# Three kept samples with y made early, their scaling shared with VectorE, and the last sample but one stored in parts

## The chip, the core and the metric

The kernel runs on one core of a Trainium2 chip. The metric is the device time of one execution in microseconds (us), that of the kernel before: 1872.82, 1877.70 and 1878.64 us in three runs, median 1877.7.

## What is computed

The input x is 32 samples of 256 channels with 56 x 56 = 3136 pixels, float32 (3136 KB a sample). Two layers follow one another, here cut to what matters:

```python
# layer 0: rotate the channels, quantise to 8 bits over ALL samples, rotate back
im = relu(x) as (256, all pixels); mn = mean(im); p = u.T @ (im - mn); p = clip(p, -cv, cv)
q  = round((p - min(p)) * 255 / (max(p) - min(p)))      # min, max per channel, over all samples
y  = u @ dequantised(q); y = y - mean(y) + mn
# layer 1: an attention weight per sample and channel, from a covariance
h = relu(w1 @ y * g + b); d = relu(w_dr @ h * g + b)    # 256 -> 256 -> 128 channels
cov = covariance of d over the sample's pixels           # 128 x 128
att = sigmoid(w_fc @ (rows of cov weighted by w_row) + b_fc)
out = y * att
```

Minimum, maximum and mean run over all 32 samples, so that nothing of layer 1 can begin before all of p is known and quantised. The output needs y twice over: once folded into h (the kernel multiplies w1 by u beforehand and works on q alone), and once as itself, scaled by att.

## The kernel before, in words

There are three stages, each a block of its own with a program for each engine.

**Stage 1** (to 564 us) computes p for all samples, with minimum and maximum. 28 samples go to a scratch in DRAM; the last four (RES = 4, the kept samples) stay in SBUF as `p_res[:, 0..3]`.

**Stage 2** (564 to 772 us) quantises p once to get the mean of q. The 28 samples come back from DRAM as 56 tiles of 128 x 3136 float32 (a channel half each, 1568 KB), through four buffers `pt`. SP loads a buffer again as soon as VectorE has quantised it (L431 to L441). VectorE quantises a tile (L633), ScalarE sums it (L525). The four kept samples are quantised too, and their q is kept as bytes (`q_kept`). Pairs of samples are numbered i = 0..13, the tiles of a pair t = 0..3. Beside this, TensorE makes y of two kept samples (MADE = 2) ahead of time, in chunks of the pixels: CH = 7 chunks of a sample with 512, 512, 512, 512, 384, 384 and 320 columns. A list `Y_PLACES` (L393) says after which tile VectorE does the work for the next chunk: `keep_y(j - 1)` copies the chunk before from PSUM to `p_res` in two halves (L606), `halve(j)` turns the bytes of chunk j into float16 for TensorE (L599). VectorE waits in `keep_y` for TensorE's eight matmuls of the chunk (L502).

**Stage 3** (from 772 us) runs the second layer, sample after sample: the four kept ones first, in the order of `ORDER`, then the 28 from DRAM, which are quantised again. A phase is one sample, with seven steps s = 0..6, one chunk each. The text counts the phases 0, 1, 2 and so on; phases 6 and later are a loop. The engines of a step work on different chunks, and each engine's order is written out:

- TensorE: z of chunk s (8 matmuls, L1024), y of the chunk 11 steps back, that is of the sample before (8 matmuls, L998), d of chunk s-1 (L949), covariance of chunk s-2 (L931). In step 1 the covariance comes right behind z. In step 4 the logits (L1009).
- ScalarE: gg of chunk s-2 (L1066), h of chunk s in two halves (L1074), hh (L1079), in step 4 the sigmoid and the scales `att_cy` (L1087, L1092), then y times att in two halves (L1112).
- VectorE: conversion of chunk s+2 (L1128, with the quantisation L1135 ahead of it for samples from DRAM), low half of g (L1182), in steps 1, 2 and 3 the small work of the covariance and the attention weights (L1210 to L1245), g (L1172) and low half of h (L1160).
- SP: in step 4 the store of a sample whose seven chunks are done (L891), and loads of the samples from DRAM.

Where y of a chunk was made in stage 2 (`made(o)`), TensorE leaves it out and ScalarE scales it in place, from SBUF to SBUF. For two made samples these are steps 4 to 6 of phase 1, all of phase 2 and steps 0 to 3 of phase 3. On such steps VectorE does g ahead of the low half of h (`has_no_y`, L1246).

The last sample has its y (`final_output`, L965) in three PSUM buffers, the first three chunks of it ahead of its logits; ScalarE and VectorE scale a half each, and SP stores chunk by chunk (L895 to L897). The sample before it is stored whole, in step 4 of phase 32 (L891).

## Time and profile before

| | |
|---|---|
| median of three runs | 1877.7 us (1872.82 to 1878.64) |
| the profiled execution | 1876.54 us, span 1874.8 us |
| TensorE busy | 90% of the span |
| VectorE busy | 83% |
| ScalarE busy | 79% |
| TensorE's mean granted clock | 0.944 of 2.4 GHz |
| DMA | 477.38 MB, 255 GB/s over the span |
| the chain that ended last | TensorE 55% of the span, VectorE 2%, ScalarE 1% |

The rows below come from the page of the profiled execution and from its trace. The chain is the chain of waits that ended last. A window is a stretch of the span, given with the busy time of each engine in it. A row of the timeline is one instruction or a few alike, with the idle time before it and what ended it in square brackets.

### The profile page before, as it was taken

The numbers are of one execution on the slowest core, as the hardware profiler recorded it, in microseconds if no ns is written. First come the engines' busy times: TensorE is split into PE (matmuls) and PEld (weight loads), VectorE is DVE, ScalarE is ACT, GpSimd is POOL, SyncE is SP. The second block draws the span as 40 slices with busy tenths as digits, with TensorE's granted clock in tenths as the row PEclk, the third lists the DMA queues.
The fourth block names the chain that finished last, engine by engine and source line by source line (L and its number), as shares of the span: only waits on it lengthen the run. The fifth ranks groups of instructions, "written<-read, shape, count | busy, mean of one in ns | idle before, by whom it ended". The sixth has DMA issues, their size and how long they took to land.

```text
span 1874.8 us, 40122 instructions
## 1 busy us (share of the span) xinstructions
PE 1693.6 (90%) x13394; PEld 1319.7 (70%) x13394; DVE 1558.2 (83%) x2855; ACT 1489.5 (79%) x2265; POOL 460.6 (25%) x136
## 2 busy tenths in 40 slices
PE   8999999999993034489999999999999999999998
PEld 8999999999992011366666666666666666666665
DVE  6888888888887787678888888888888888888885
ACT  7777777777768997689878878888788788887885
POOL 7888888888870000000000000000000000000000
PEclk9999999999995556699999999999999999999999
DMA  9998998999999999503546546455464464554635
GB/s 338 372 376 304 375 365 315 373 351 328 374 356 386 429 431 429 231 2 148 170 158 236 169 173 219 158 211 189 156 235 168 174 217 159 213 188 154 235 116 207
DMA packets 140592, 477.38 MB, mean 255 GB/s; under 512 B 10624, under 2 KB 33536, under 8 KB 125568
## 3 DMA queue, kind: packets, MB, share of 16 engines
q1 hardware_dynamic: 140544, 476.75, 68.9%
q8 instruction: 28, 0.46, 0.1%
q14 instruction: 20, 0.16, 0.0%
HBM read 284.04 MB, written 192.68 MB: 254 GB/s over the span
## 4 chain that ended last, share of the span: by engine, by line
PE 55%; DVE 2%; ACT 1%; issue 1%; ACTq 0%; DVEq 0%
PE z_ps L1024 17%; PE y_ps L998 16%; PE d_ps L949 14%; PE cov_ps L931 5%; PE ch_ps L1009 1%; DVE hl L1160 0%; ACT p_res L1112 0%; DVE g L1172 0%; PE ch_ps L962 0%; PE ch_ps L961 0%; DVE gg L1182 0%; ACT h L1074 0%; PE y_ps L978 0%; ACT gg L1066 0%; PE cov_ps L934 0%
## 5 line engine op out<-in xcount | busy, mean ns | idle before, releaser
L299 POOL TENSOR_TENSOR xl<-early,xh 128x1568 fp32r<-128x1568 f32 x128 | 459.7, 3592 | 96.1 <-ACT xh L258 96.1
L1024 PE MATMUL z_ps<-qr,wh 128*128 128x512 f16 (+2 forms) x896 | 315.4, 355 | 0.0
L1024 PE MATMUL z_ps<-qr,wl 128*128 128x512 f16 (+2 forms) x896 | 315.4, 355 | 0.0
L1160 DVE TENSOR_TENSOR hl<-h,hh 128x1024 f16<-128x1024 f32 (+2 forms) x224 | 243.9, 1089 | 79.8 <-ACT hh L1079 79.5
L258 ACT ACTIVATE xh<-early 128x1568 fp32r<-128x1568 f32 x128 | 194.2, 1517 | 139.1 <-PE pp L316 139.0
L949 PE MATMUL d_ps<-vh,hh 128*128 128x128 f16 x1600 | 281.1, 220 | 3.5 <-DVE hl L1160 3.3
L998 PE MATMUL y_ps<-qr,udh 128*128 128x512 f16 (+2 forms) x812 | 283.9, 353 | 0.0
L998 PE MATMUL y_ps<-qr,udl 128*128 128x512 f16 (+2 forms) x812 | 283.6, 352 | 0.0
L1074 ACT ACTIVATE h<-z_ps,sb_h 128x512 f32<-128x512 f32 (+2 forms) x448 | 264.4, 626 | 23.2 <-PE z_ps L1024 20.4
L949 PE MATMUL d_ps<-vh,hl 128*128 128x128 f16 x1600 | 281.1, 220 | 0.0
L949 PE MATMUL d_ps<-vl,hh 128*128 128x128 f16 x1600 | 281.0, 220 | 0.0
L316 PE MATMUL pp<-xh,uh 128*128 128x392 f32 x1024 | 267.1, 342 | 9.1 <-ACT xh L258 9.1
L1112 ACT ACTIVATE p_res<-y_ps,att_cy 128x512 f32<-128x512 f32 x406 | 269.6, 713 | 6.5 <-ACT att_cy L1092 5.0
L316 PE MATMUL pp<-xh,ul 128*128 128x392 f32 x1024 | 266.3, 341 | 0.0
L1066 ACT ACTIVATE gg<-g 128x512 f16<-128x512 f32 (+1 forms) x224 | 130.7, 584 | 160.7 <-DVE g L1172 160.5
L350 DVE TENSOR_REDUCE pmin<-pp 128x784 f32 x256 | 248.3, 970 | 0.0
L1079 ACT ACTIVATE hh<-h 128x1024 f16<-128x1024 f32 (+2 forms) x224 | 213.0, 951 | 7.1
L252 ACT ACTIVATE early<-early 128x784 f32<-128x784 f32 x256 | 215.3, 844 | 3.6 <-DMA early<-in_x_dram 3.6
L316 PE MATMUL pp<-xl,uh 128*128 128x392 f32 x1024 | 204.5, 341 | 0.0
L316 PEld LDWEIGHTS pp<-xh,uh 128*128 128x128 f32 x1024 | 188.5, 188 | 9.1 <-issue 9.1
L316 PEld LDWEIGHTS pp<-xh,ul 128*128 128x128 f32 x1024 | 188.6, 188 | 0.0
L316 PEld LDWEIGHTS pp<-xl,uh 128*128 128x128 f32 x1024 | 185.1, 188 | 0.0
(197 smaller groups left out, 2961.1 us busy)
## 6 DMA issues: line engine op xcount, KB each, us to landing
early<-in_x_dram SPq DMA_DIRECT2D x128, 784.0 KB, 6.7
out_dram<-p_res SPq DMA_DIRECT2D x31, 3136.0 KB, 10.2
early<-p_scratch SPq DMA_DIRECT2D x42, 1568.0 KB, 12.8
p_res<-p_scratch SPq DMA_DIRECT2D x112, 512.0 KB, 4.4
p_scratch<-early SPq DMA_DIRECT2D x56, 784.0 KB, 7.7
p_scratch<-late SPq DMA_DIRECT2D x56, 784.0 KB, 7.7
p_res<-p_scratch SPq DMA_DIRECT2D x56, 384.0 KB, 3.2
late_tile<-p_scratch SPq DMA_DIRECT2D x13, 1568.0 KB, 12.8
```

Of the source, the lines that this page charges most:

```text
L252: last = nc.scalar.activation(xs[:, k, m], xs[:, k, m], ACT.Relu, accum_out=xsum[:, m, bass.ds(g, 1)])
L258: nc.scalar.activation(xh[:, k % 2], xs[:, k], ACT.Copy).then_inc(high_done, 1)
L299: nc.gpsimd.tensor_tensor(xl[:, k % 2], xs[:, k], xh[:, k % 2].bitcast(F32), ALU.subtract).then_inc(split_done, 1)
L316: last = nc.tensor.matmul(pp[:, k % 2, m, c, 0:SC], lhs, rhs[:, c * SC:(c + 1) * SC], start=first and n == 0, stop=final and n == len(part ...
L350: nc.vector.tensor_reduce(pmin[:, m, bass.ds(g, 1)], p_psum(k, m), AX_XY, ALU.min).then_inc(psum_read, 1)
L949: last = nc.tensor.matmul(d_ps[:, par, t], lhs, rhs, start=n == 0, stop=n == len(parts) - 1)
L998: last = nc.tensor.matmul(y_ps[:, m, 0:widths[c]], part[:, k, m * P:(m + 1) * P], qr[:, slot, k, columns(c)], start=k == 0 and part is udh ...
L1024: last = nc.tensor.matmul(z_ps[:, m, 0:w], part[:, k, m * P:(m + 1) * P], qr[:, a, k, columns(s)], start=k == 0 and part is wh, stop=k == ...
L1074: nc.scalar.activation(h32[:, par, m, 0:w], z_ps[:, m, 0:w], ACT.Relu, bias=sb_h[:, m:m + 1]).then_inc(z_read, 1)
L1079: nc.scalar.activation(hh[:, par, :, 0:w], h32[:, par, :, 0:w], ACT.Copy).then_inc(hh_done, 1)
L1112: nc.scalar.activation(yo[:, slot, m, columns(c)], y_in, ACT.Identity, scale=att_cy[:, m, 0:1], bias=att_cy[:, m, 1:2]).then_inc(y_free, 1)
L1160: nc.vector.tensor_tensor(hl[:, par, :, 0:w], h32[:, par, :, 0:w], hh[:, par, :, 0:w], ALU.subtract).then_inc(h_split, 1)
```

## The change

- MADE goes from 2 to 3. `ORDER` becomes [1, 3, 2, 0]: y of kept samples 1, 3 and 2 is made in stage 2. `Y_PLACES` gets 22 places from pair 5 to pair 12 (before, 15 were used, from pair 6 to the first tile of pair 12). In pairs 10 and 12 all four tiles are places.
- Made chunks are scaled by ScalarE (first half of the channels) and by VectorE (second half, in place, behind the low half of h). A semaphore `made_scaled` counts VectorE's part; SP waits for it ahead of the store, and ScalarE ahead of the sigmoid, which overwrites `att_cy`.
- A made sample is stored from its place in `p_res`. The first one lies in `p_res[:, 1]`, which is also the buffer of the samples from DRAM (`pc`). So the first seven chunk loads move from the start of stage 3 to phase 2, step 4, behind the store of that sample and a wait for its landing.
- The third chunk of the last sample's y moves behind the logits.
- The last sample but one is stored in three parts (chunks 0 to 2, 3 and 4, 5 and 6), each as soon as it is scaled, and no more whole in phase 32.

```diff
--- before.py
+++ after.py
@@ -389,9 +389,11 @@
         tiles = [tiles_in_all // CH + (c < tiles_in_all % CH) for c in range(CH)]
         starts = [P * sum(tiles[:c]) for c in range(CH)]
         widths = [min(P * t, M - at) for t, at in zip(tiles, starts)]
-        MADE = 2
-        Y_PLACES = [(i, t) for i in range(6, PAIRS) for t in ((0, 2) if i <= 2 * RES else (0, 1, 2))][1:]
-        ORDER = [*range(RES - MADE, RES), *range(RES - MADE)]
+        MADE = 3
+        Y_PLACES = [(i, t) for i in range(5, 2 * RES + 1) for t in (0, 2)] + [
+            (i, t) for i in range(2 * RES + 1, PAIRS - 1) for t in range(3 + (i % 2 == 0))]
+        ORDER = [1, 3, 2, 0]
+        assert len(ORDER) == RES and len(Y_PLACES) > MADE * CH
 
         def columns(c):
             return slice(starts[c], starts[c] + widths[c])
@@ -764,7 +766,7 @@
         cov_centred, r_summed, r_done = sem("cov_centred"), sem("r_summed"), sem("r_done")
         weighted_done = sem("weighted_done")
         logits_done, att_done, attb_done = sem("logits_done"), sem("att_done"), sem("attb_done")
-        y_done, y_free = sem("y_done"), sem("y_free")
+        y_done, y_free, made_scaled = sem("y_done"), sem("y_free"), sem("made_scaled")
         half_free = [sem(f"half_free{m}") for m in range(K)]
 
         with ExitStack() as c_:
@@ -843,6 +845,10 @@
 
                 return not has(r2, a, s, CH + Y_LAG) or made(output_chunk(r2, a, s)[0])
 
+            def kept_y(o, c):
+
+                return p_res[:, ORDER[o // CH], :, columns(c)]
+
             def converted_chunk(r2, a, s):
 
                 return 2 * r2 + a + (s + LEAD) // CH, (s + LEAD) % CH
@@ -864,9 +870,6 @@
             def _(sp):
                 def load(i, c):
                     sp.dma_start(pc[:, :, columns(c)], p0_v[i, :, :, columns(c)]).then_inc(chunk_loaded[c], 16)
-
-                for c in range(CH):
-                    load(0, c)
 
                 def store(n, a, first, end):
 
@@ -878,7 +881,12 @@
                             sp.wait_ge(half_free[m], end)
                     else:
                         sp.wait_ge(y_free, K + K * (CH * n + end))
-                    sp.dma_start(out_v[which, :, :, part], yo[:, a, :, part]).then_inc(out_stored[a], 16)
+                    if isinstance(n, int) and n < MADE:
+                        sp.wait_ge(made_scaled, CH * n + end)
+                        source = p_res[:, ORDER[n], :, part]
+                    else:
+                        source = yo[:, a, :, part]
+                    sp.dma_start(out_v[which, :, :, part], source).then_inc(out_stored[a], 16)
 
                 def phase(r2, a):
                     for s in range(CH):
@@ -887,15 +895,23 @@
                             n, c = converted_chunk(r2, a, s)
                             sp.wait_ge(chunk_quantised, CH * (n - RES) + c + 1)
                             load(n - RES + 1, c)
-                        if s == Y_LAG and exists(r2, a, back=2) and exists(r2, a, back=1):
+                        if s == Y_LAG and exists(r2, a, back=2) and exists(r2, a):
                             store(2 * r2 + a - 2, a, 0, CH)
+                            if isinstance(r2, int) and 2 * r2 + a == 2:
+
+                                sp.wait_ge(out_stored[0], 32)
+                                for c in range(CH):
+                                    load(0, c)
 
                 phases(sp, phase)
 
+                parts_before = [(0, 3), (3, 5), (5, CH)]
+                for first, end in parts_before:
+                    store(N - 2, 0, first, end)
                 last_parts = [(c, c + 1) for c in range(CH)]
                 for first, end in last_parts:
                     store(N - 1, 1, first, end)
-                sp.wait_ge(out_stored[0], 16 * (N // 2) + 16)
+                sp.wait_ge(out_stored[0], 16 * (N // 2 - 1 + len(parts_before)) + 16)
                 sp.wait_ge(out_stored[1], 16 * (N // 2 - 1 + len(last_parts)) + 16)
 
             @block.tensor
@@ -985,7 +1001,7 @@
                     if has(r2, a, s, CH + Y_LAG):
                         o, slot, c = output_chunk(r2, a, s)
                         if final(o):
-                            for n in range(0, 3) if c == 0 else range(c + 2, min(c + 3, CH)):
+                            for n in range(0, 2) if c == 0 else range(c + 2, min(c + 3, CH)):
                                 final_output(FINAL + n, n)
                             return
                         if made(o):
@@ -1038,6 +1054,8 @@
                         if not exists(r2, a):
                             spread(r2, a, s)
                         logits(r2, a, s)
+                        if s == Y_LAG and has(r2, a, s, CH + Y_LAG) and final(output_chunk(r2, a, s)[0]):
+                            final_output(FINAL + 2, 2)
                         reduced(r2, a, s)
                         if s != 1:
                             covariance(r2, a, s)
@@ -1083,6 +1101,8 @@
                             act.wait_ge(logits_done, n)
 
                             act.wait_ge(y_free, K + K * (first_chunk(r2, a) - CH))
+                            if isinstance(r2, int) and 2 <= n <= MADE + 1:
+                                act.wait_ge(made_scaled, CH * (n - 1))
                             for m in range(K):
                                 last = nc.scalar.activation(att[:, m:m + 1], ch_ps[:, 2 * P + m:2 * P + m + 1],
                                                             ACT.Sigmoid, bias=bfc_sb[:, m:m + 1])
@@ -1103,14 +1123,15 @@
                                                      ACT.Identity, scale=att_cy[:, 0, 0:1],
                                                      bias=att_cy[:, 0, 1:2]).then_inc(half_free[0], 1)
                                 continue
+                            if made(o):
+                                kept = kept_y(o, c)[:, 0]
+                                nc.scalar.activation(kept, kept, ACT.Identity, scale=att_cy[:, 0, 0:1],
+                                                     bias=att_cy[:, 0, 1:2]).then_inc(y_free, K)
+                                continue
                             for m in range(K):
-                                if made(o):
-                                    y_in = yo[:, slot, m, columns(c)]
-                                else:
-                                    act.wait_ge(y_done, K * (o - MADE * CH) + m + 1)
-                                    y_in = y_ps[:, m, 0:widths[c]]
-                                nc.scalar.activation(yo[:, slot, m, columns(c)], y_in, ACT.Identity,
-                                                     scale=att_cy[:, m, 0:1],
+                                act.wait_ge(y_done, K * (o - MADE * CH) + m + 1)
+                                nc.scalar.activation(yo[:, slot, m, columns(c)], y_ps[:, m, 0:widths[c]],
+                                                     ACT.Identity, scale=att_cy[:, m, 0:1],
                                                      bias=att_cy[:, m, 1:2]).then_inc(y_free, 1)
 
                 phases(act, phase)
@@ -1246,6 +1267,12 @@
                         if has_no_y(r2, a, s):
                             rectified_g(r2, a, s)
                             low_half_of_h(r2, a, s)
+                            if has(r2, a, s, CH + Y_LAG):
+                                o, slot, c = output_chunk(r2, a, s)
+                                kept = kept_y(o, c)[:, 1]
+                                dve.wait_ge(attb_done, o // CH + 1)
+                                nc.vector.tensor_scalar(kept, kept, att_cy[:, 1, 0:1], att_cy[:, 1, 1:2], ALU.mult,
+                                                        ALU.add).then_inc(made_scaled, 1)
                         else:
                             low_half_of_h(r2, a, s)
                             if has(r2, a, s, CH + Y_LAG) and final(output_chunk(r2, a, s)[0]):
```

## Rows read from the trace of the kernel before

In a row of windows stand: the stretch, its length, the busy time and the instructions of PE, PEld, DVE, ACT and POOL, the granted clock as a share of 2.4 GHz, the DMA share and GB/s.

**Rows 1.** Page, part 2: DMA busy in tenths, 40 slices of the span.
```profile
DMA  9998998999999999503546546455464464554635
```

**Rows 2.** Two windows of stage 2.
```profile
600.00:640.00 40.00, 2.66 (x6) 1.43 (x6) 30.29 (x34) 40.00 (x30) 0.00 (x0) 0.50 1.01 430
...
720.00:740.00 20.00, 10.90 (x35) 3.94 (x36) 17.37 (x20) 14.82 (x11) 0.00 (x0) 0.67 1.01 428
```

**Rows 3.** Timeline of VectorE in stage 2, around one 512-column chunk of y.
```profile
716.35 1.91 DVE L633 TENSOR_SCALAR qt<-early,lo,qa 128x3136 uint8<-128x3136 f32 x1
...
720.02 0.69 DVE L606 COPY p_res<-wfc_ps 128x512 f32<-128x512 f32 x1 [1.01 <-PE wfc_ps L502]
...
721.23 1.91 DVE L633 TENSOR_SCALAR qt<-early,lo,qa 128x3136 uint8<-128x3136 f32 x1
```

**Rows 4.** Timeline of VectorE in stage 2 where no y work is left.
```profile
754.54 1.91 DVE L633 TENSOR_SCALAR qt<-late_tile,lo,qa 128x3136 uint8<-128x3136 f32 x1 [1.80 <-DMA late_tile<-p_scratch]
```

**Rows 5.** Page, part 6: loads of stage 2, KB each, median us to landing.
```profile
late_tile<-p_scratch SPq DMA_DIRECT2D x13, 1568.0 KB, 12.8
```

**Rows 6.** Windows of phases 1 to 4 of stage 3.
```profile
801.31:830.32 29.01, 24.41 (x267) 17.67 (x266) 23.48 (x48) 22.85 (x38) 0.00 (x0) 1.00 0.01 2
830.32:860.50 30.18, 26.22 (x267) 18.83 (x266) 23.59 (x48) 27.85 (x47) 0.00 (x0) 0.94 0.26 107
860.50:893.16 32.66, 30.75 (x291) 20.92 (x290) 26.07 (x53) 29.85 (x49) 0.00 (x0) 0.95 0.36 130
893.16:927.18 34.02, 34.02 (x322) 23.31 (x321) 29.58 (x62) 27.92 (x46) 0.00 (x0) 1.00 0.50 174
```

**Rows 7.** Windows of steps: phase 1 steps 1-3, phase 2 steps 1-3, phase 4 steps 0-3.
```profile
804.45:817.28 12.83, 11.68 (x126) 8.09 (x124) 11.58 (x30) 9.09 (x13) 0.00 (x0) 1.00 0.00 1
...
833.74:848.88 15.14, 13.31 (x124) 9.24 (x123) 11.49 (x30) 13.62 (x21) 0.00 (x0) 0.89 0.00 1
...
893.16:913.09 19.93, 19.93 (x189) 13.45 (x187) 17.66 (x43) 15.99 (x24) 0.00 (x0) 1.00 0.34 96
```

**Rows 8.** The chain of waits in phase 2, steps 0 to 2: start, us, what.
```profile
834.81 0.87 ACT p_res L1112 x2
...
836.21 0.52 ACT gg L1066
...
838.01 2.49 PE d_ps L949 x24
```

**Rows 9.** Group by shape: ScalarE scales made halves, phases 1 to 3.
```profile
L1112 ACT ACTIVATE p_res<-p_res,att_cy 128x512 f32<-128x512 f32 x16 | 12.1, 802 | 0.1
```

**Rows 10.** Group by shape: VectorE quantises 512 columns, from phase 4 on.
```profile
L1135 DVE TENSOR_SCALAR q<-p_res,lo,qa 128x512 uint8<-128x512 f32 x212 | 105.6, 540 | 0.0
```

**Rows 11.** Windows: 3.4 us of phase 2 at the lower clock; the end.
```profile
838.20:841.60 3.40, 3.40 (x27) 2.58 (x25) 1.68 (x6) 2.30 (x4) 0.00 (x0) 0.50 0.02 5
1850.00:1855.00 5.00, 4.91 (x36) 2.88 (x32) 2.51 (x11) 3.60 (x6) 0.00 (x0) 1.00 0.01 2
1857.00:1872.00 15.00, 9.46 (x53) 5.02 (x51) 5.74 (x9) 5.64 (x11) 0.00 (x0) 1.00 1.03 411
```

**Rows 12.** The chain of waits at the end: start, us, what.
```profile
1858.81 1.73 PE d_ps L978 x8
1860.54 0.35 PE ch_ps L1009 x4
...
1865.91 1.30 PE d_ps L978 x8
1867.21 1.10 PE y_ps L978 x8
...
1868.33 0.61 DVE p_res L1257
```

**Rows 13.** Timeline of SP: its last issue, the last chunk's store.
```profile
1869.02 0.70 SPq L881 DMA_DIRECT2D out_dram<-p_res  x1
```

**Rows 14.** DMA issues at the end: that store's KB and us to landing.
```profile
out_dram<-p_res SPq DMA_DIRECT2D x1, 320.0 KB, 5.3
```

## What is predicted, and why

> **What bounds the kernel now.** I read the page's slices first. The DMA share tells the stages apart: about 9 tenths in stages 1 and 2, about 5 in stage 3 [rows 1]. Then windows by stage. In stage 2 the DMA engines are busy without a break at 429 GB/s while TensorE has much idle time; ScalarE is fully busy for a while, but later it is not and the DMA still is [rows 2]. Where no y work is left, VectorE waits 1.80 us for each tile [rows 4]. So stage 2 ends when 28 samples have been read, and work on VectorE there is free as long as no load is issued late. In stage 3 the windows by phase show two regimes [rows 6]. From phase 4 on TensorE is busy for the whole 34.02 us of a phase: it is the bound. In phases 1 to 3, where y has been made, TensorE is busy only 24.4 to 30.8 us of 29.0 to 32.7. There the chain of waits goes round the engines: ScalarE's scaling of made y (L1112), behind it gg, behind that VectorE and TensorE's d [rows 8]. At the end the chain is TensorE, the logits, the scaling, and the DMA engines are saturated from 1857 to 1872 after standing nearly idle before 1855 [rows 11].
>
> **The third made sample: what TensorE saves.** Y of a 512-column chunk takes TensorE 1.73 us, of a 384 one 1.30, of the 320 one 1.10 [rows 12]. A sample is 4 x 1.73 + 2 x 1.30 + 1.10 = 10.6 us of matmuls that leave stage 3. But a phase without y does not get 10.6 us shorter: phase 2 takes 30.2 us against 34.0 of phase 4 [rows 6]. So the question is how long made phases are after the change, when ScalarE scales one half instead of two.
>
> **ScalarE and VectorE in made steps.** A half of 512 columns costs ScalarE 0.80 us by duration [rows 9]. One half goes, so gg, h and hh of the next step start some 0.75 us earlier. VectorE gets an operation the trace does not have: 128x512 float32, SBUF to SBUF, two scalars per partition. The nearest row is the quantisation of the same shape from the same memory, 0.54 us [rows 10]; as such operations overlap at their edges, I take 0.45 from start to start. The bounds are 0.3 and 0.8, the latter being what ScalarE takes for this shape [rows 9]. The row's 0.54 us is for float32 read and bytes written. The Trainium skill, VectorE: DVE Perf Modes, section "The perf-mode tier table", gives a one-source float32 operation within SBUF the doubled rate, 1227 ns for 2048 elements; by it an estimate for 512 is some 0.35 us, and the sum would be 1 to 2 us better than mine.
>
> Now the steps. In steps 1 to 3 VectorE also has the covariance work. Phase 1 shows these three steps with no scaling of y at all: 12.83 us, VectorE busy 11.58 of them, so VectorE is nearly the bound [rows 7]. Phase 2, with both halves on ScalarE, has 15.14, part of it at the lower clock (0.89 in the mean) [rows 7]. After the change I take 12.83 + 3 x 0.45 = 14.2. The other four steps of phase 2 were 30.18 - 15.14 = 15.0; the shorter ScalarE should give 0.3 of it. A made phase then takes 28.9 us.
>
> Phase by phase, against [rows 6]:
> - Phase 1 has three steps with made chunks, and ScalarE is shorter in them: 29.0 to 28.3.
> - Phase 2: 30.2 to 28.9.
> - Phase 3 becomes fully made, but its last two steps have the first quantisations of a sample from DRAM, 2 x 2 x 0.45 = 1.8 us on VectorE [rows 10], of which I charge 1.4: 32.7 to 30.3.
> - Phase 4: its first four steps lose y, and TensorE's 19.93 us would fall by 4 x 1.3 to 1.7. But VectorE is busy for 17.66 us of them [rows 7]; with four more operations of 0.54 that is 19.8, so VectorE takes over as the bound and nearly nothing is won: 34.0 to 33.9.
>
> Together 125.9 us become 121.4, a gain of 4.5 us. The steps of phase 1 that I built on ran at the full clock, those of phases 2 and 3 had a fall to the lower clock each (means 0.94 and 0.95) [rows 6]. In one such stretch the granted clock was 0.50 for 3.4 us, that is 1.2 GHz, behind a stall of TensorE, and 24 matmuls of d took 2.49 us [rows 8, 11]. I charge one fall, 1.2 us (at most half of 3.4, 1.7, less what the waits absorb). Stage 3's body: -3.3 us; between -7 (no fall, the cheap operation) and +1 (three falls, the dear one).
>
> **What the seven more chunks cost in stage 2.** Each brings VectorE one L599 and two L606, about 1.9 us, 13 us in all. The cover is the DMA: a tile takes 1568 KB at 429 GB/s = 3.74 us, and VectorE quantises it in 1.9 [rows 2 to 4]. Where places follow one another without a gap, VectorE also waits for TensorE at the lower clock: the row pair shows a tile with a 512-column chunk taking 721.23 - 716.35 = 4.9 us, 1.0 of it waiting [rows 3]. That is 1.15 us late per such tile; 384- and 320-column chunks are about even. In pair 10 to 12 there are up to seven places in a row; walking through them with these numbers VectorE is up to 3.1 us late at tile (11,3) and on time again in pair 13. How late may it be? A load lands 12.8 us after its issue, three others being ahead of it [rows 5]; so the DMA engines have 3 x 3.74 - 1.9 = 9.3 us of work left when VectorE is on time. 3.1 is well under that. I take 0.5 us for unevenness among the DMA engines, bounds 0 and 3.
>
> **What is moved on SP.** The seven chunk loads leave the start of stage 3, where nothing waits for them, and now stand behind the store of the first made sample and a wait for its landing. Behind that wait on SP are those loads and the store in phase 3, step 4. The store begins in step 4 of phase 2, takes about 11 us, the loads 3.2 MB / 429 GB/s = 7.5 and seven issues; VectorE wants the first chunk in step 5 of phase 3, a phase and a step later, some 32 us. Slack over 10 us: nothing. The cover gone, each us late would stall VectorE and then TensorE. ScalarE's new wait ahead of the sigmoid: behind it stand the sigmoid and the scaling, then gg. VectorE's last half of step 3 ends before ScalarE's hh of step 4, so nothing.
>
> **The end.** With the third final chunk behind the logits, these start 1.73 us earlier [rows 12]; its y is still ready when the third scaling wants it. Everything to the last scaling (1868.33 + 0.61) moves by 1.7. The last store was issued at 1869.02 and landed 5.3 us later, at 1874.3 [rows 13, 14], because the DMA engines still had the whole of sample 30 to write at 1857 [rows 11]. In parts, more than half of it goes into the idle time before 1855. The last sample alone needs 3.2 MB / 411 GB/s = 7.8 us from about 1862: to 1870, plus the landing's tail of some 2 us. Gain 2.3 us, between 1.5 and 3.5.
>
> **The sum**, against the profiled execution (1876.54; span 1874.8): -3.3 + 0.5 - 2.3 = -5.1, that is 1871.4. The median of the runs is 1.2 above that execution, their mean 0.1 below it; I lay half between and say 1872.0. About 0.3% (5.6 us) is what a measurement of this kernel can tell from no change, and my gain is right at it.
>
> **The rivals.**
> 1. The gain is eaten in the made phases. TensorE's clock is at 0.50 where it had stalled [rows 8, 11], and the change makes a third phase of that kind. The Trainium skill says so too, TensorE: Matmul & The Clock Gate, section "HAM oscillation — how this bites in real kernels": waits between bursts of matmuls bring the clock down again and again; the trace agrees, with 3.4 us at 0.50. With a fall in each of three phases (3.6 us) and VectorE's operation at 0.8, the body gives +0.5, the end -2.3, stage 2 +0.5: 1875. For it: both whole made phases before had a fall. Against: the stall that came ahead of it hangs on ScalarE's second half.
> 2. Nearly all goes well: no fall, the cheap operation, the end at 3.5: -10 us, 1867. Against it: VectorE's 17.66 of 19.93 us in phase 4.
> 3. Slower: stage 2 turns from DMA-bound to VectorE-bound. If VectorE's lateness in pairs 9 to 12 passes 9.3 us, buffers are freed too late, the DMA engines run dry, and each further place costs its full 1.9 us: up to 13 us for seven, less the 5.6 of the rest: +7, 1884. Against it: the walk ends at 3.1.
> 4. The split of the work does not show: made phases stay at 30.2 since another chain (hl to d to g to gg) is as long, while the rest is as forecast: 1875 as well. I count it with the first.
>
> **How the numbers follow.** Forecast 0.55 (its own range 1869 to 1875.5), rivals 1 and 4 0.25, rival 2 0.13, rival 3 0.07. The range to be given reaches from 1866.5 to 1877.5; it takes in rivals 1, 2 and 4 and leaves out rival 3 and the edges. Faster by over 0.3% (below 1872.1): rival 2 and somewhat over half of the forecast, 0.45. Slower by over 0.3%: rival 3 and little else, 0.07. Same: 0.48.
>
> **What would show it.** Windows of the phases: made phases 28 to 29.5, phase 4 about 34 with VectorE at 0.9 and more in its first steps. L599 and L606 seven and fourteen more, stage 2 no longer, the DMA share still 1.01 in pairs 9 to 12. The logits 1.7 us earlier against the end of the last d, the last store landing some 3 us after its issue. The prediction is wrong if the DMA share falls in stage 2, if VectorE waits for a chunk load in phase 3, or if made phases stay over 30 us.

## The result

The changed kernel takes 1867.77 us in the median of nine runs (1865.97 to 1869.84), the kernel before 1875.35 in its nine (1872.32 to 1880.25). The ratio is 0.9952, 95% interval 0.9942 to 0.9962: some 9 us, between 7 and 11; the two medians are 7.6 us apart. Forecast were 5.7 us from a median of 1877.7, that is 1872.0, with 0.48 of the chance on no difference that can be measured. The sign of the forecast sum was right, its size too small, and the largest single chance lay on "same", where the time did not come out. The measured 1867.8 us lies outside the forecast's own range (1869 to 1875.5) and inside the range given (1866.5 to 1877.5) only because that took in the second rival.

The profiled execution of the changed kernel has a span of 1866.5 us, 8.3 less than that of before. First the page, granted clock, DMA share and groups of the chain:

```profile
PEclk9999999999996567699999999999999999999999
DMA  9998998998999999405546546455465464554535
```
```profile
PE 51%; DVE 4%; ACT 0%; issue 0%; DVEq 0%; ACTq 0%
```

The stages are as in [rows 1]. In the chain ScalarE has gone and VectorE has come up from 2 to 4%. Now the windows of phases 1 to 4 in the changed kernel, columns as in [rows 6]:

```profile
802.03:830.47 28.44, 24.40 (x266) 17.65 (x265) 24.38 (x50) 22.22 (x37) 0.00 (x0) 1.00 0.01 2
830.47:858.74 28.27, 24.49 (x268) 17.73 (x266) 26.04 (x55) 23.29 (x40) 0.00 (x0) 1.00 0.26 110
858.74:889.05 30.31, 24.47 (x266) 17.71 (x265) 28.01 (x59) 23.99 (x40) 0.00 (x0) 1.00 0.61 228
889.05:922.71 33.66, 29.61 (x292) 20.11 (x290) 31.96 (x68) 25.94 (x42) 0.00 (x0) 1.00 0.53 185
```

Together 120.7 us against 125.9 in [rows 6], 5.2 less. The clock column (TensorE's granted clock as a share of 2.4 GHz) reads 1.00 in all four, where it read 0.94 and 0.95 in phases 2 and 3: there the clock had fallen to 0.50 for 3.4 us each time. Such a stretch is called a fall below. VectorE is busy 32.0 of 33.7 us in phase 4. The steps that answer to [rows 7] are phase 2 steps 1 to 3 and phase 4 steps 0 to 3:

```profile
833.62:847.41 13.79, 11.84 (x125) 8.10 (x123) 12.58 (x32) 11.06 (x17) 0.00 (x0) 1.00 0.00 1
889.05:908.14 19.09, 15.34 (x157) 10.25 (x155) 18.71 (x45) 13.94 (x20) 0.00 (x0) 1.00 0.41 122
```

The new operation, by shape (busy us, mean ns), where [rows 10] had stood in for it:

```profile
L1274 DVE TENSOR_SCALAR p_res<-p_res,att_cy 128x512 f32<-128x512 f32 x12 | 6.5, 543 | 0.5 <-ACT att_cy L1112 0.5
```

The end, as the chain of waits (start, us, what), for [rows 12]; SP's issues of the first and the last chunk of sample 31, for [rows 13]; and the last store's size and us to landing, for [rows 14]:

```profile
1854.45 0.35 PE ch_ps L1025 x4
...
1856.62 1.90 PE y_ps L994 x8
...
1861.13 1.10 PE y_ps L994 x8
...
1862.25 0.61 DVE p_res L1284
```
```profile
1856.68 0.37 SPq L889 DMA_DIRECT2D out_dram<-p_res  x1
...
1862.94 0.37 SPq L889 DMA_DIRECT2D out_dram<-p_res  x1
```
```profile
out_dram<-p_res SPq DMA_DIRECT2D x1, 320.0 KB, 3.1
```

From the logits to the end of the span are 1866.5 - 1854.45 = 12.05 us; before, 1874.8 - 1860.54 = 14.26. And from the first z of phase 5 to the logits are 931.74 us against 933.36. So the end gives 1.6 + 2.2 = 3.8 us.

The 8.3 us then are: start of stage 3 at 775.28 instead of 774.91, +0.4; phase 0 26.75 instead of 26.40, +0.3 (both vary by 2 us and more between traces whatever the change, see the section on stage 2); phases 1 to 4 -5.2; the end -3.8.

### The profile page after: what moved, and what is told of

Read it like the earlier page. It is cut to its first block, busy times and chain, and to the rows that moved or that the text cites. A ratio compares the mean times of both kernels' runs of the same rounds, so it can differ in the third digit from the quotient of the medians.

```text
span 1866.5 us, 40162 instructions
## 1 busy us (share of the span) xinstructions
PE 1695.2 (91%) x13394; PEld 1317.1 (71%) x13394; DVE 1576.0 (84%) x2897; ACT 1475.6 (79%) x2244; POOL 460.2 (25%) x136
## 4 chain that ended last, share of the span: by engine, by line
PE 51%; DVE 4%; ACT 0%; issue 0%; DVEq 0%; ACTq 0%
PE y_ps L1014 16%; PE z_ps L1040 16%; PE d_ps L965 13%; PE cov_ps L947 5%; DVE hl L1181 1%; DVE gg L1203 1%; PE ch_ps L1025 1%; DVE g L1193 0%; DVE p_res L1274 0%; DVE qr L1149 0%; PE ch_ps L978 0%; PE ch_ps L977 0%; DVE q L1156 0%; PE y_ps L994 0%; PE cov_ps L950 0%
## 5 line engine op out<-in xcount | busy, mean ns | idle before, releaser
L1014 PE MATMUL y_ps<-qr,udh 128*128 128x512 f16 (+2 forms) x784 | 274.1, 353 | 0.0
L1014 PE MATMUL y_ps<-qr,udl 128*128 128x512 f16 (+2 forms) x784 | 273.8, 352 | 0.0
L1133 ACT ACTIVATE p_res<-y_ps,att_cy 128x512 f32<-128x512 f32 x392 | 260.2, 712 | 6.5 <-ACT att_cy L1112 5.0
```

The lines of the kernel that those rows point to most:

```text
L1014: last = nc.tensor.matmul(y_ps[:, m, 0:widths[c]], part[:, k, m * P:(m + 1) * P], qr[:, slot, k, columns(c)], start=k == 0 and part is udh ...
L1133: nc.scalar.activation(yo[:, slot, m, columns(c)], y_ps[:, m, 0:widths[c]], ACT.Identity, scale=att_cy[:, m, 0:1], bias=att_cy[:, m, 1:2]) ...
```

## The experiments

Two questions are open: whether the 5.2 us of the phases come from the third sample, from the shared scaling or from the clock; and why the end gave 3.8 instead of 2.3. A few us of spread lie over all times, so that each run is read from its trace first, phase by phase; its ratio to the kernel before stands beside it. There is one trace of each run.

### The end, one edit undone at a time

`whole_store`, the changed kernel with the last sample but one stored whole:

```diff
-                parts_before = [(0, 3), (3, 5), (5, CH)]
+                parts_before = [(0, CH)]
```

> The changed kernel with the last sample but one stored whole again. Theory (the backlog at the end is what costs): the last scaling stays where it is, but the last store lands late, behind sample 30: after the first logits of the end some 14.2 us pass instead of 12.05, so the kernel takes 2.2 us more than the changed one, 1870.0. Rival (the prediction's own term, 0.6 us: the last sample's 3.2 MB bound the end in any case): 0.6 us more.

Measured: 0.9974 of the kernel before (0.9965 to 0.9984). Logits to end is 1871.9 - 1856.06 = 15.8 us, 3.8 more than in the changed kernel: more than either expectation (2.2 and 0.6). Without the parts the whole gain of the end is gone. The last store lands 6.0 us after its issue:

```profile
out_dram<-p_res SPq DMA_DIRECT2D x1, 3136.0 KB, 10.7
...
out_dram<-p_res SPq DMA_DIRECT2D x1, 320.0 KB, 6.0
```

`third_first`, the changed kernel with the third final chunk ahead of the logits:

```diff
-                            for n in range(0, 2) if c == 0 else range(c + 2, min(c + 3, CH)):
+                            for n in range(0, 3) if c == 0 else range(c + 2, min(c + 3, CH)):
...
-                        if s == Y_LAG and has(r2, a, s, CH + Y_LAG) and final(output_chunk(r2, a, s)[0]):
-                            final_output(FINAL + 2, 2)
```

> The changed kernel with the third final chunk ahead of the logits again. Theory (the end is a chain through the logits): 1.7 us more than the changed kernel, and the last store still lands some 3 us after its issue. Rival (the DMA engines bound the end once the parts are stored early, and start the same): 0 to 0.5 us more.

Measured: 0.9973 (0.9963 to 0.9983). The logits come 933.5 us after the start of phase 5 (931.7 in the changed kernel), 1.7 later (1856.41 - 922.93 = 933.48); from them to the end it is 12.0 us, and the last store again lands in 3.1 us. The trace has it as the theory did. The ratios of this run and of the changed kernel are 3.9 us apart, more than 1.7, but each is uncertain by some 2.

`order_only`, the kernel before with that edit alone, the other way round: the third chunk goes behind the logits, and sample 30 is still stored whole.

> The kernel before with only the third final chunk behind the logits; the last sample but one is stored whole. Theory (the DMA engines, which still write sample 30, bound the end): the logits are 1.6 us earlier, and logits to end grows by as much, from 14.3 to 15.9 us: no gain. Rival (my prediction's step: everything to the end moves with the logits): 1.7 us less, logits to end stays at 14.3.

Measured: 1.0002 (0.9990 to 1.0013), nothing, though a gain of 1.7 us is only just at the edge of the interval; the trace decides it. The logits are 1.8 us earlier (1860.35 - 928.83 = 931.5 us after phase 5 began, instead of 933.4), and logits to end is 1876.2 - 1860.35 = 15.9 us: all but 0.2 given back. The DMA engines show why, in two windows of its end (columns as in rows 2):

```profile
1859.50:1874.00 14.50, 8.52 (x48) 4.47 (x46) 5.02 (x7) 5.64 (x11) 0.00 (x0) 0.89 1.01 401
1874.00:1876.20 2.20, 0.00 (x0) 0.00 (x0) 0.00 (x0) 0.00 (x0) 0.00 (x0) 0.50 0.05 19
```

The DMA share is 1.01 until 1874, while the last scaling was over at 1868.15 + 0.61. Sample 30, written whole from its last scaling on, and sample 31 behind it fill the engines; when the last chunk is scaled matters little. The backlog reaches back to SP: in order_only its last issue begins 1.1 us after the last scaling is over and takes 1.16 us, where in the changed kernel it begins after 0.08 us and takes 0.37.

```profile
1869.86 1.16 SPq L881 DMA_DIRECT2D out_dram<-p_res  x1
```

`tail_only`, the kernel before with both edits of the end.

> The kernel before with nothing but the two edits at the end (third final chunk behind the logits, last sample but one in three parts). Theory (the end is apart from the rest and worth what the traces show): 3.8 us less than the kernel before. Rival (my forecast of the end): 2.3 us less.

Measured: 0.9977 (0.9967 to 0.9986), 4.3 us, the interval from 2.6 to 6.2. From the first z of phase 5 to the end of the span the traces have: neither edit 947.6 us (before), the order alone 947.4 (order_only) and 947.6 (whole_store), the parts alone 945.5 (third_first), both 943.8 (changed kernel) and 943.7 (tail_only). The six traces shown further down that have both edits have 943.6 or 943.7 as well, and before_again, with neither, 948.0. The parts alone are worth 2.1, the order 0 to 0.2 without them and 1.7 with them.

### Which part shortens the phases

`scalar_scales`, the changed kernel with both halves on ScalarE; the two waits for VectorE's part, which are not shown here, go too:

```diff
...
-                                kept = kept_y(o, c)[:, 0]
-                                nc.scalar.activation(kept, kept, ACT.Identity, scale=att_cy[:, 0, 0:1],
-                                                     bias=att_cy[:, 0, 1:2]).then_inc(y_free, K)
+                                for m in range(K):
+                                    kept = kept_y(o, c)[:, m]
+                                    nc.scalar.activation(kept, kept, ACT.Identity, scale=att_cy[:, m, 0:1],
+                                                         bias=att_cy[:, m, 1:2]).then_inc(y_free, 1)
...
-                                nc.vector.tensor_scalar(kept, kept, att_cy[:, 1, 0:1], att_cy[:, 1, 1:2], ALU.mult,
-                                                        ALU.add).then_inc(made_scaled, 1)
```

> The changed kernel, three samples made, but ScalarE scales both halves as before. Theory A (ScalarE's second half is what made the made phases long and brought the falls of the clock): phases 2 and 3 take 30.2 and 31.5 us or more instead of 28.3 and 30.3, falls of the clock come back, 4 to 6 us more than the changed kernel. Theory B (the share brings little, the third sample brings the gain by taking matmuls away): at most 1 us more.

Measured: 0.9960 (0.9946 to 0.9974), some 1.5 us above the changed kernel, which the intervals don't separate. Windows of phases 1 to 4 in its trace:

```profile
801.84:830.82 28.98, 24.39 (x266) 17.65 (x265) 23.45 (x48) 22.82 (x38) 0.00 (x0) 1.00 0.01 2
830.82:860.98 30.16, 26.23 (x268) 18.65 (x266) 23.67 (x48) 27.84 (x47) 0.00 (x0) 0.94 0.27 109
860.98:891.84 30.86, 26.08 (x266) 18.28 (x265) 25.50 (x52) 28.51 (x48) 0.00 (x0) 0.94 0.61 228
891.84:924.46 32.62, 29.55 (x291) 20.11 (x289) 30.06 (x63) 28.80 (x48) 0.00 (x0) 1.00 0.53 182
```

Neither theory alone. The falls are back in phases 2 and 3 and these are 1.9 and 0.6 us longer, as A has it. But phase 4 is 1.0 us shorter than in the changed kernel: there VectorE's share costs. In sum +1.9, not the 4 to 6 of theory A, nor the 1 at most of theory B.

`two_made`, the changed kernel with `MADE = 2`.

> The changed kernel with MADE = 2: scaling shared, end changed, but only two samples made. Theory A: the third sample is worth little, because VectorE bounds the steps that it frees: phases 1 to 4 take 28.4, 28.3, 31.5 and 34.0 us, 1.5 us more than the changed kernel. Theory B: the third sample is worth a whole phase without y, some 5 us more. Stage 2 would be 0 to 0.4 us shorter by both.

Measured: 0.9961 (0.9948 to 0.9973). Phases 28.44, 28.26, 31.02 and 34.02, together 121.7, 1.1 us more than with three. Theory A: the third sample, 10.6 us of matmuls, is worth about one once the scaling is shared. The four traces make a table: neither edit 125.9 us (before), the share alone 121.7 (two_made), the third sample alone 122.6 (scalar_scales), both 120.7. So each alone is worth 4.1 and 3.2, and on top of the other 1.9 and 1.1. The 4.1 and the 1.9 hold two falls of the clock each.

`double_scale` does VectorE's scaling of a made half twice, first into a spare tile:

```diff
+                                spare = prod[:].rearrange("p j c -> p (j c)")[:, 0:widths[c]]
+                                nc.vector.tensor_scalar(spare, kept, att_cy[:, 1, 0:1], att_cy[:, 1, 1:2], ALU.mult,
+                                                        ALU.add)
```

> The changed kernel with VectorE's scaling of a made half done twice (the first time into a spare tile), 21 more operations. Theory (VectorE is the bound in steps 1 to 3 of made phases and in steps 0 to 3 of phase 4, has slack in the others): some 11 to 13 of the 21 cost 0.45 us each, 5 to 6 us more. Rival (a chain through several engines bounds these steps, VectorE waits in it): 2 us more or less.

Measured: 0.9994 (0.9985 to 1.0003). Windows of phases 2 to 4:

```profile
830.78:861.38 30.60, 24.98 (x266) 17.76 (x265) 28.96 (x62) 23.73 (x39) 0.00 (x0) 1.00 0.25 106
861.38:894.06 32.68, 25.00 (x268) 17.76 (x265) 30.97 (x66) 23.73 (x39) 0.00 (x0) 1.00 0.61 215
894.06:929.76 35.70, 29.60 (x292) 20.12 (x290) 33.99 (x73) 26.06 (x42) 0.00 (x0) 1.00 0.49 168
```

Phases 1 to 4 take 127.9 us, 7.2 more instead of the 5 to 6 expected: 0.34 us for each of the 21 operations, of the 0.46 that one of 512 columns takes from start to start in the chain. So VectorE is the bound in more of the made steps than I had counted: there is little slack on it in phases 2 and 3 (2.3 and 2.4 us more for seven operations each) and none in the first steps of phase 4 (2.0 us for four).

### The clock

`before_again` is the kernel before, unchanged, for the clock of each execution.

> The kernel before, unchanged, for the granted clock of each execution beside its time. Theory (falls of the clock in phases 2 and 3 are part of its time and differ between executions): the mean clock varies by 0.003 and more, and executions with the lower clock are 1 to 4 us longer. Rival (the spread has another cause): no relation between clock and time.

Measured: 1.0005 (0.9995 to 1.0016). Over 60 executions of the kernel before, these included, the mean granted clock runs from 0.942 to 0.949, the time from 1872.4 to 1880.3 us; those at 0.945 and below have medians of 1878.7 to 1879.0, those at 0.947 and above of 1872.8 to 1874.1, and the correlation is -0.79. So most of the spread of this kernel goes with its clock. That the falls of the phases make it is not shown: the two groups are 5 to 6 us apart, with a fall worth about 1 (below), and the mean clock also holds stage 2 and phase 0, where the clock differs between traces too. The phases 1 to 3 of the new profile:

```profile
801.97:831.78 29.81, 25.73 (x268) 18.80 (x266) 23.62 (x49) 23.65 (x39) 0.00 (x0) 0.94 0.01 2
831.78:860.11 28.33, 24.40 (x267) 17.66 (x266) 23.35 (x48) 26.81 (x46) 0.00 (x0) 1.00 0.27 115
860.11:891.73 31.62, 29.08 (x290) 20.11 (x289) 25.99 (x53) 29.62 (x49) 0.00 (x0) 1.00 0.36 135
```

Here there is one fall, in phase 1, and phase 3 without one takes 31.6 instead of 32.7 us, with the same stall ahead of it (below); tail_only and order_only repeat the two values. A fall in phase 3 costs 1.0 us. In phases 1 and 2 the price is not as clear. Both profiles have one fall there: in phase 1 it costs that phase 0.8 us and phase 2 then takes 28.3, together 58.1; in phase 2 the two phases take 59.2. No trace of a kernel with the phases of the kernel before has neither. Phases 1 to 4 together take 123.8 us here, against 125.9 with two falls, so that against this execution the changed kernel would have gained 3.1 us in them and not 5.2.

`share_two_steps`: VectorE's share only in steps 0 and 1 of phases 2 and 3, ScalarE scales both halves elsewhere. A function `vector_half(o)` says which; the waits count accordingly:

```diff
+            def vector_half(o):
+
+                return o < 2 * CH and o % CH in (3, 4)
```

> VectorE's share only in steps 0 and 1 of phases 2 and 3, four operations instead of 21; elsewhere ScalarE scales both halves. Theory (the falls hang on the one stall of TensorE in step 1, which ScalarE's second half in step 0 lengthens): no fall in stage 3, phases 1 to 4 take 29.0, 28.3, 29.8 and 32.6 us, 1.0 us less than the changed kernel. Rival (the share is needed in all steps to keep the clock up): falls come back, phases 2 and 3 take 30 us and more as with ScalarE alone, 1 us or more above the changed kernel.

Measured: 0.9952 (0.9937 to 0.9967).

```profile
802.08:831.07 28.99, 24.40 (x266) 17.66 (x265) 23.46 (x48) 22.84 (x38) 0.00 (x0) 1.00 0.01 2
831.07:860.37 29.30, 24.62 (x267) 17.68 (x265) 24.34 (x50) 26.33 (x45) 0.00 (x0) 1.00 0.28 112
860.37:890.35 29.98, 24.45 (x268) 17.69 (x265) 26.16 (x54) 27.02 (x46) 0.00 (x0) 1.00 0.63 234
```

Four operations instead of 21, and no fall; but this is one trace, and it does not prove that step 1 was the cause. The idle times of TensorE in front of the covariance, called stalls here, say more. They are the number in brackets; first the kernel before, then before_again, then share_two_steps and the changed kernel:

```profile
826.39 0.28 PE L931 MATMUL cov_ps<-gg 128*128 128x257 f16 x1 [2.02 <-DVE gg L1182]
837.37 0.28 PE L931 MATMUL cov_ps<-gg 128*128 128x257 f16 x1 [1.75 <-DVE gg L1182]
867.55 0.28 PE L931 MATMUL cov_ps<-gg 128*128 128x257 f16 x1 [1.75 <-DVE gg L1182]
```
```profile
827.04 0.28 PE L931 MATMUL cov_ps<-gg 128*128 128x257 f16 x1 [2.01 <-DVE gg L1182]
838.01 0.28 PE L931 MATMUL cov_ps<-gg 128*128 128x257 f16 x1 [1.20 <-DVE gg L1182]
867.15 0.28 PE L931 MATMUL cov_ps<-gg 128*128 128x257 f16 x1 [1.74 <-DVE gg L1182]
```
```profile
827.15 0.28 PE L955 MATMUL cov_ps<-gg 128*128 128x257 f16 x1 [2.02 <-DVE gg L1217]
837.89 0.28 PE L955 MATMUL cov_ps<-gg 128*128 128x257 f16 x1 [1.51 <-DVE gg L1217]
```
```profile
826.44 0.28 PE L947 MATMUL cov_ps<-gg 128*128 128x257 f16 x1 [1.36 <-DVE gg L1203]
```

The kernel before fell behind the second and third of its stalls, before_again behind the first. [rows 11] have the first of these falls; the windows of the other two are:

```profile
868.91:872.32 3.41, 3.41 (x20) 1.97 (x17) 2.18 (x4) 2.39 (x5) 0.00 (x0) 0.50 0.02 5
```
```profile
828.39:831.80 3.41, 3.41 (x29) 2.65 (x27) 2.37 (x5) 3.38 (x7) 0.00 (x0) 0.50 0.01 2
```

In the five traces in which ScalarE scales both halves throughout phases 1 to 3 (before, before_again, tail_only, order_only, scalar_scales) there are 13 stalls of 1.74 to 2.02 us, and 8 falls, each beginning 0.8 to 1.7 us behind the end of one of them. share_two_steps has one of 2.02 us and two of 1.51, and no fall. In the seven traces with the share in all made steps of phases 1 to 3 there is no fall; six of them have no stall over 1.5 us in phases 1 to 4, double_scale has two, 1.79 and 1.73 us. So the share removes the stalls that a fall can follow, also one in step 5 of phase 1 that I had not looked at; which of them are followed by one differs from execution to execution. The sum of phases 1 to 4 was 120.9 instead of the 119.7 that I had expected: phase 2 is 1.0 us longer than with the share in all its steps. So the share does shorten made steps as such, too.

`share_to_phase_3` has `return o < 2 * CH + 3`: the share everywhere but in phase 4.

> The changed kernel, but in phase 4 (made steps 0 to 3) ScalarE scales both halves; VectorE's share stays in phases 1 to 3. Theory (VectorE's operation lengthens phase 4, where it also quantises; the share is only worth having where it keeps the clock up): phases 1 to 3 as in the changed kernel (28.4, 28.3, 30.3), phase 4 32.6 instead of 33.7, no fall of the clock in stage 3: 1.0 us less than the changed kernel. Rival (phase 4 then has a stall and a fall of its own): no gain.

Measured: 0.9950 (0.9936 to 0.9965), median 1866.84 us.

```profile
857.83:888.13 30.30, 24.47 (x267) 17.72 (x265) 27.99 (x59) 24.02 (x40) 0.00 (x0) 1.00 0.62 227
888.13:920.57 32.44, 29.56 (x292) 20.12 (x289) 30.44 (x64) 27.90 (x46) 0.00 (x0) 1.00 0.55 193
```

Phase 4 gets its 1.2 us back and the other phases keep theirs, 119.4 in all. It is the shortest of these kernels by its phases; its ratio cannot be told from that of the changed kernel.

### Stage 2

`no_y_in_two` leaves out all work on y in stage 2 (the call of `y_work` and TensorE's loop).

> The changed kernel without any work on y in stage 2: no halving, no matmuls, no copies; stage 3 scales what lies in the kept places, so that three samples' output is not y. Theory (the DMA engines bound stage 2, the y work is hidden but for some unevenness): stage 3 starts 0 to 0.5 us earlier than in the changed kernel. Rival (VectorE's lateness costs): it starts 1 to 3 us earlier.

Measured: 0.9946 (0.9932 to 0.9960). Window from 749 us to the first z, and phase 0:

```profile
749.00:774.36 25.36, 1.73 (x8) 1.73 (x9) 15.48 (x15) 18.70 (x16) 0.00 (x0) 0.50 0.75 316
774.36:798.99 24.63, 24.02 (x236) 16.57 (x237) 18.63 (x27) 18.05 (x26) 0.00 (x0) 0.92 0.01 1
```

The first z comes at 774.36 instead of 775.28, 0.9 us earlier; but with the y work of three samples it comes anywhere between 775.2 and 776.5 (777.3 in whole_store), for the most part since stage 2 does not begin at the same time in every trace. From VectorE's first quantisation of stage 2 to the first z it is 774.36 - 569.64 = 204.7 us, against 775.28 - 569.39 = 205.9 in the changed kernel (205.9 to 206.1 in six of the seven traces with the same work, 206.9 in one), 205.3 with two made samples (two_made) and 205.5 to 205.9 in the four traces with the stage 2 of the kernel before. So all 21 chunks cost 1.2 us, more than the theory has and at the lower edge of the rival, and the third sample's seven 0.6 at most. Phase 0 is 2.1 us shorter, but that isn't shown to be the y work: it takes 24.2 to 24.6 us in four of the thirteen traces and 26.2 to 26.8 in the rest, whatever the kernel, with a mean clock of 0.92 here and 0.82 in the changed kernel. The shorter ones are those in which the clock had risen earlier. How VectorE waits in stage 2 is as foreseen; a tile with a 512-column chunk, places one after another, in the changed kernel:

```profile
733.36 1.91 DVE L635 TENSOR_SCALAR qt<-early,lo,qa 128x3136 uint8<-128x3136 f32 x1
...
737.10 0.69 DVE L608 COPY p_res<-wfc_ps 128x512 f32<-128x512 f32 x1 [0.99 <-PE wfc_ps L504]
...
738.31 1.91 DVE L635 TENSOR_SCALAR qt<-early,lo,qa 128x3136 uint8<-128x3136 f32 x1
```

4.95 us from tile to tile, with 1.0 of waiting, as in [rows 3]; the DMA share of 700 to 760 us stays at 1.00 and 1.01.

## Why the prediction was wrong in size

- **The phases by their steps: right.** Forecast 28.3, 28.9, 30.3 and 33.9 us, measured 28.4, 28.3, 30.3 and 33.7. The stand-in of 0.54 us for the unseen operation was 0.543. The estimate from the Trainium skill, VectorE: DVE Perf Modes, section "The perf-mode tier table", was 0.35 us; the trace doesn't agree. The operation took 543, 475 and 442 ns for 512, 384 and 320 columns, 0.53 ns a column. By that slope the 1227 ns that the same section of the Trainium skill gives for 2048 elements make an estimate of 0.42 us for 512, so that 0.35 was too low even by it. double_scale shows that the price matters. That VectorE takes over in phase 4 was right as well (busy 18.7 of 19.1 us in its first four steps).
- **The fall of the clock: the first step that failed.** "I charge one fall, 1.2 us." None came, neither here nor in any other trace with the share. The price was about right (1.0 us in phase 3), the number wrong. I had noted in the first rival that the stall hangs on ScalarE's second half, and then did not use it; and I looked at two stalls of three. Two falls were in the time of the profiled kernel before, and both went. That there were two is partly luck: other executions of that kernel have one. The 1.2 us charged for nothing, with 0.7 us from phases that came out a little shorter, make 1.9 of the 3.2 us between forecast sum (-5.1) and trace (-8.3).
- **The end: the second step that failed**, and the larger surprise in its mechanism. "Everything to the last scaling moves by 1.7 [...] Gain 2.3." I took the 1.7 from the logits as given and the parts as an extra of 0.6, from "7.8 us from about 1862: to 1870, plus the landing's tail of some 2 us". order_only shows the first to be worth nothing by itself: the DMA engines bound the end. The term of the parts was 2.1, not 0.6, and only behind it the 1.7 count. The measured 3.8 lies outside the range that I gave the end (1.5 to 3.5) and is 1.5 us of the 3.2. In the forecast's own terms, counted from the first z of phase 5 and set on the time axis of the kernel before, the first store of sample 31 is issued at 1861.15 and not at 1862, 0.85 us of the 1.5, and the last one lands 9.4 us later, not 9.8; a store that meets no backlog lands in 3.1 us, all told.
- **Stage 2: right.** Forecast +0.5, measured +0.4, at the first z as well as from the first quantisation on; the whole y work costs 1.2. The +0.3 in phase 0 is within what phase 0 varies by.
- **SP's moved loads and ScalarE's new wait: right**. In phases 2 to 4 no engine waits for a load, nor ScalarE for VectorE's part of the scaling; only SP itself waits, 8.8 us for the landing of the first store.
- **The rivals.** Falls in every made phase (rival 1) are refuted by the seven traces with the whole share in phases 1 to 3 (of the "both whole made phases" named for it, phase 3 was made in its first four steps only), slower through stage 2 (rival 3) by the DMA share, and made phases that stay at 30.2 us (rival 4) by the 28.3 of phase 2. The rule that stood beside rival 1 (the Trainium skill, TensorE: Matmul & The Clock Gate, "HAM oscillation — how this bites in real kernels") agrees with the traces of the kernel before in that the clock falls behind waits, there of 1.74 us and more; in the changed kernel waits between bursts are still there, up to 1.48 us, and it does not fall. What came is nearest to rival 2, but not by its reasons: the operation was not cheap and VectorE was the bound. That the time came out near rival 2's 1867 is luck so far as its reasons go. The chances were drawn to the border of 0.3%, on which the forecast happened to lie, so that 1.9 and 1.5 us of error, both to the same side, sufficed to put the largest chance on the wrong outcome.

How the 5.2 us of the phases divide depends on the order in which the edits are counted (the table at two_made). A fall less is worth 1.0 us in phase 3, and two are gone; what the other was worth isn't shown by itself. The share beyond the four operations of share_two_steps brings 1.3 us in phases 1 to 3 (88.3 there, 87.0 in share_to_phase_3). The third sample brings 0.7 in phase 3 and 0.4 in phase 4 where the scaling is shared (two_made), 1.8 and 1.4 where it is not (scalar_scales); VectorE's share costs 1.0 to 1.2 us in phase 4. That the falls come of the stalls is supported, not proven, by their order in time in eight cases and by six traces with neither; why other stalls of the same length (five here, two in double_scale, one in share_two_steps) were not followed by a fall stays open. The split of the 5.2 us is that of single traces, though the phases repeat within 0.1 us in traces with the same edits and the same falls; in the ratios, scalar_scales and the changed kernel are 1.5 us apart within intervals that overlap.

## What to carry to other kernels

When two edits shorten the same end, ask for each what bounds it without the other: here an earlier result was worth nothing while transfers queued up in front of its store, and the idle DMA time just ahead of the end was the place to put them. Work taken off the bounding engine pays only up to the next engine's load: 10.6 us of matmuls bought 1.1 us with the shared scaling and 3.2 without, because in phase 4 of the kernel before VectorE was busy for 0.87 and ScalarE for 0.82 of the time already. And before summing, look whether a phase of the profile taken as a base holds a fall of the clock; it belongs to a term of its own, with the stall that came ahead of it.

## What the runs showed of the hardware

- In phases 1 to 4 of the thirteen traces TensorE's granted clock fell to 0.50, that is 1.2 GHz, for 3.4 us behind 8 of 16 waits of TensorE of 1.73 to 2.02 us, and never behind one of 1.51 us or less; in phase 3, 1.0 us was lost by it. With the scaling shared the chain in step 1 of phase 2 is as follows, and d runs at the full clock (24 matmuls in 1.46 us, against 2.49 in [rows 8]):

```profile
834.20 1.23 DVE hl L1181
835.43 0.46 DVE p_res L1274
835.89 0.48 DVE gg L1203
...
837.06 1.46 PE d_ps L965 x24
```

- Stores of the same 320 KB landed in 3.1 us with no backlog, 5.3 and 6.0 us behind a whole sample, and in order_only the last one landed 2 us after the DMA share had dropped to 0.05. Issuing a store took SP 0.37 us with no backlog, and 1.16 and 1.21 us for the last one of order_only and whole_store.
- VectorE's scaling of 128 x 512 float32 in place, with two scalars per partition, took 543 ns, and 0.46 us from start to start; ScalarE took 802 ns for the same half [rows 9].
